# Products of the two layers of a conv mixture of experts: alternating by nine matmuls in place of by 27

## The reference, cut to what matters

```python
B, C, H, W = (32, 384, 28, 28)
E, HID, K = (4, 384, 2)
scores = jax.nn.softmax(x_flat @ gate_w + gate_b, -1)
top_v, top_i = jax.lax.top_k(scores, K)
top_w = jax.nn.softmax(top_v, -1)
...
coef = jnp.einsum('ke,kbhw->ebhw', present.astype(x.dtype), wmap)
hdn = jax.nn.relu(jnp.einsum('bchw,edc->ebdhw', x, w1) + b1[:, None, :, None, None])
y = jnp.einsum('ebdhw,eod->ebohw', hdn, w2) + b2[:, None, :, None, None]
out = jnp.einsum('ebohw,ebhw->bohw', y, coef)
...
x = x + _L0_conv_ref(_gn(x), ...)
```

## Time and profile before

| | |
|---|---|
| time, median of 3 runs | 2565.67 us (2565.27 to 2566.45) |
| time of the profiled execution | 2567.38 us |
| its span, first to last instruction | 2565.6 us |
| granted TensorE clock, mean | 0.996 |
| PE busy | 2519.3 us (98%), 13266 matmuls |
| DVE busy | 1623.8 us (63%) |
| ACT busy | 630.7 us (25%) |
| HBM | 73 GB/s over the span |

### The profile page before, as it was taken

How to read it: one execution, slowest core, us unless ns; L and a number is a source line. 1 busy time by engine, 2 the same in 40 slices (tenths; PEclk the granted TensorE clock), 3 DMA queues, 4 the chain that set the end, 5 groups by cost and what they waited for, 6 DMA issues and landing times.

```text
span 2565.6 us, 34840 instructions
## 1 busy us (share of the span) xinstructions
PE 2519.3 (98%) x13266; PEld 2302.0 (90%) x13266; DVE 1623.8 (63%) x3293; ACT 630.7 (25%) x973; POOL 74.4 (3%) x44
## 2 busy tenths in 40 slices
PE   4899999999999999999999999999999999999999
PEld 3799999999999999999999999999999999999998
DVE  7766666666666657665666666576666666665643
ACT  3322222222222222222222222222222222222211
POOL 3000000000000000000000000000000000000000
PEclk9999999999999999999999999999999999999999
DMA  4322123222133221232311322203322123231120
GB/s 161 89 78 71 52 70 89 78 82 59 52 89 93 67 79 55 69 100 68 92 55 46 100 78 82 80 25 97 89 71 78 51 72 100 61 91 51 46 75 22
DMA packets 193439, 190.15 MB, mean 74 GB/s; under 512 B 29808, under 2 KB 191856, under 8 KB 193264
## 3 DMA queue, kind: packets, MB, share of 16 engines
q1 hardware_dynamic: 193264, 187.81, 25.7%
HBM read 146.03 MB, written 41.75 MB: 73 GB/s over the span
## 4 chain that ended last, share of the span: by engine, by line
PE 96%; DVE 2%; DMA 1%; issue 1%; POOL 0%; ACT 0%; SPq 0%; DVEq 0%; POOLq 0%; ACTq 0%
PE y_ps L479 16%; PE y_ps L481 16%; PE z_ps L460 16%; PE y_ps L480 16%; PE z_ps L462 16%; PE z_ps L461 16%; PE g_ps L344 1%; DMA b_sb<-in_b 0%; DMA rows<-rows_dram 0%; DVE h_lo L519 0%; DVE x_part L323 0%; DVE x_lo L335 0%; POOL w_lo L847 0%; DVE x_raw L303 0%; DMA rows_dram<-wrow 0%
## 5 line engine op out<-in xcount | busy, mean ns | idle before, releaser
L508 DVE SCALAR_TENSOR_TENSOR hid<-z_ps,b_sb,rows 128x448 f32<-128x448 f32 x668 | 453.5, 679 | 753.9 <-PE z_ps L462 739.7
L479 PE MATMUL y_ps<-h_lo,w_hi 128*128 128x448 f32 x2016 | 741.8, 368 | 13.4 <-DVE h_lo L519 13.1
L460 PE MATMUL z_ps<-x_lo,w_hi 128*128 128x448 f32 x2016 | 743.4, 369 | 1.3 <-DVE x_lo L335 1.0
L481 PE MATMUL y_ps<-h_hi,w_hi 128*128 128x448 f32 x2016 | 741.1, 368 | 0.0
L480 PE MATMUL y_ps<-h_hi,w_lo 128*128 128x448 f32 x2016 | 740.9, 368 | 0.0
L462 PE MATMUL z_ps<-x_hi,w_hi 128*128 128x448 f32 x2016 | 736.7, 365 | 0.0
L461 PE MATMUL z_ps<-x_hi,w_lo 128*128 128x448 f32 x2016 | 736.5, 365 | 0.0
L515 ACT ACTIVATE h_hi<-hid 128x448 fp32r<-128x448 f32 x672 | 385.2, 578 | 1356.8 <-DVE hid L508 1343.2
L519 DVE SCALAR_TENSOR_TENSOR h_lo<-hid,h_hi 128x448 fp32r<-128x448 f32 x672 | 413.6, 616 | 26.5 <-ACT h_hi L515 26.1
L479 PEld LDWEIGHTS y_ps<-h_lo,w_hi 128*128 128x128 f32 x2016 | 379.3, 188 | 50.4 <-DVE h_lo L519 14.4
L460 PEld LDWEIGHTS z_ps<-x_lo,w_hi 128*128 128x128 f32 x2016 | 379.9, 188 | 38.0 <-issue 7.1
(11 more groups left out here) (97 smaller groups left out, 695.6 us busy)
## 6 DMA issues: line engine op xcount, KB each, us to landing
rows<-rows_dram SPq DMA_DIRECT2D x78, 560.0 KB, 7.4
x_raw<-in_x SPq DMA_DIRECT2D x62, 588.0 KB, 7.4
res<-in_x SPq DMA_DIRECT2D x80, 336.0 KB, 3.5
out<-res SPq DMA_DIRECT2D x78, 336.0 KB, 3.1
rows<-rows_dram SPq DMA_DIRECT2D x16, 840.0 KB, 7.2
res<-in_x SPq DMA_DIRECT2D x16, 504.0 KB, 5.8
out<-res SPq DMA_DIRECT2D x16, 504.0 KB, 6.0
rows<-rows_dram SPq DMA_DIRECT2D x16, 280.0 KB, 6.6
```

The source lines that it names most:

```text
L460: nc.tensor.matmul(z, w1_hi[:, e, j, ks], lo, start=(j == 0), stop=False)
L479: nc.tensor.matmul(y, w2_hi[:, e, k, ms], h_lo[:, slot], start=first, stop=False)
L481: ins = nc.tensor.matmul(y, w2_hi[:, e, k, ms], h_hi[:, slot], start=False, stop=last)
L508: nc.vector.scalar_tensor_tensor(hid[:, q % HIDS], z_ps[:, q % ZB, 0:T], b1_sb[:, e, k:k + 1], coef, ALU.add, ALU.mult).then_inc(scaled, 1)
```

## The change

`mm2` takes the chunks that it is to do, and PE's loop goes over chunks: nine matmuls of `mm1` for chunk c of unit u + 1, and then nine of `mm2` for chunk c of unit u. unit_done is still signalled after a unit's last matmul. Lines behind the edit move up by one (`add_product` is L534 before and L533 after).

```diff
-        def mm2(pe, G, u):
+        def mm2(pe, G, u, chunks):
             t, e = divmod(u, E)
             tail = G.last and u == UNITS - 1
...
-            for k in range(NK):
+            for k in chunks:
...
-            if tail:
-                return
-            ins.then_inc(unit_done, 1)
+                if k == NK - 1 and not tail:
+                    ins.then_inc(unit_done, 1)
...
-                    if u < UNITS - 1:
-                        if not (G.first and u == 0):
-                            mm1(pe, G, u + 1, chunks=range(2 if G.first and u == 1 else 0, NK))
-                    elif not G.last:
-                        mm1(pe, after, 0)
-                    mm2(pe, G, u)
+                    for c in range(NK):
+                        if u == UNITS - 1:
+                            if not G.last:
+                                mm1(pe, after, 0, chunks=[c])
+                        elif not (G.first and (u == 0 or u == 1 and c < 2)):
+                            mm1(pe, G, u + 1, chunks=[c])
+                        mm2(pe, G, u, [c])
```

## The result

The alternating kernel takes 2606.7 us (median of 4 runs, 2604.68 to 2607.51) against 2565.47 for the kernel before: a ratio of 1.0156, 95% interval 1.0144 to 1.0169. The forecast was 2606. The profiled execution has a span of 2605.7 us.

The account below looks back on a forecast made before the run. PE was taken as the bound, going from matmul to matmul without waits. Border waits of 15.3, 11.3 and 8.8, the first group's 3.7 and clock's 1.6 made 40.7 us on 2565.67: 2606 us, range 2590 to 2626 (8 in 10).

Parts of the forecast that it names:

- The mechanism: At tile borders PE's next product waits for DVE's add_product, late behind preparation: 2596 to 2616 us, 68 in 100.
- The waits: PE at borders into tiles 1, 2 and 5: 2.18, 1.41 and 1.25 us each, about 23 times.
- C: DVE's time from scale of a tile's third chunk to add_product: 4.84, 4.07, 3.91 us; PE waits C - 2.66.
- the term of 0.83 us: At a border, PE's product starts 0.83 us behind the start of a late add_product.
- the first group: At its border into tile 1, PE does nine matmuls instead of 27 before its wait; 18 left cost 3.7 us.
- The clock: After the first group's wait of 4 us, 3.2 us at half clock lose 1.6 us; nothing at other waits.
- the clock falls at every wait in tile 1: Rival: half clock after each wait in tile 1, 2617 us, or 2628 if down twice as long; 10 in 100.
- the 1.72 us: PE idle ahead of 76.58 in the start, after which the clock stayed at 1.00; other waits were taken as nearer this.
- The pace: Speed of matmuls following each other on PE: no change, about 10 us each way; rivals faster 10, slower 8 in 100.
- The rival on the other side: DVE finishes work ahead of add_product in time at tile borders, so no waits: 2560 to 2568 us, 4 in 100.

Follow-up runs that it names:

- the first experiment: Alternating kernel with DVE's preparation ahead of add_product (tiles 1 to 6) done in the next chunk, behind add_product: 2563.74 us, ratio 0.9987 to the kernel before.
- the fourth: Alternating kernel with one more DVE reduction of 1152 elements ahead of add_product in tiles 3, 4 and 6: 2628.98 us, ratio 1.0245 to the kernel before.
- the third: Alternating kernel put back to 27 and 27 except in each tile's first unit, which alternates by nine: 2573.76 us, ratio 1.0025 to the kernel before.
- the sixth: Alternating kernel with the two products yielding to each other after three matmuls in place of nine: 2754.74 us, ratio 1.0744 to the kernel before.
- the second experiment: Alternating kernel with PE back to 27 and 27 in each tile's first unit only: 2564.6 us, ratio 0.9991 to the kernel before.
- the seventh: Kernel before (27 and 27) with DVE's preparation put behind add_product: 2566.01 us, ratio 1.0000 to the kernel before.

## Why the prediction was right

- **The mechanism** was right: nothing but `add_product` behind DVE's preparation. The first experiment takes that work away and the loss goes; the fourth adds some and it grows; the third leaves work and distance and gives z early, and it goes; the sixth follows the same reckoning.
- **The waits** were forecast as 23 in tiles 1, 2 and 5, and 23 there are. C was right within 0.03 us in all three borders shown; in tile 1 it is 4.72 us, not 4.87, in four of the seven groups. The size was a little high, because the term of 0.83 us from the start of `add_product` to the product was read from the one case there was, in the first group. There and in the last group, which is also written out, it is 0.83 after the change too; in the six groups of the loop it is 0.74. So the three waits shown are 2.16, 1.37 and 1.16 us (the gaps less 0.20), not 2.18, 1.41 and 1.25. In the sum: 34.5 us by the waits' view, of which 30.6 lie behind the first group; this view counts from the modelled end of a matmul, 0.17 us later than its follower could start, so 22 x 0.17 = 3.7 more, 34.3 us. 35.4 were forecast.
- **The first group** lost its 18 matmuls, 3.7 us, as forecast: PE has nine behind it at 113.44 where it had 27 at 115.69.
- **The clock** was the mis-sized term. 1.6 us were put down for one stretch of 3.2 us; there were two stretches, the first twice as long. 15 matmuls in the 5.46 us from 113.44 and 10 in 3.2 us: at 0.2046 us each they would take 3.07 and 2.05, so the stretches cost an estimated 2.4 + 1.2 = 3.6 us. The second stretch is the rival "the clock falls at every wait in tile 1", come true once in seven: the waits there, of up to 2.0 us, were not as safe as the 1.72 us that they were likened to.
- **The pace** was put at no change, with 10 us each way, and changed by far less: the second experiment alternates in three quarters of the units at no cost, and the windows of the seventh point to a gain of some 2 us.
- **What the sum leaves.** 34.3 + 3.7 + 3.6 = 41.6, and the spans differ by 40.1. The two executions differ already at the start: PE's first matmul, ahead of any alternation, comes after a wait for ACT of 22.2 us before and of 18.5 us after. Counted from the first product of tile 1 (115.69 and 113.44) to the end, they take 2449.9 and 2492.3 us, which is 42.4 us more and leaves 0.8. One term that the forecast lacked is larger than that: the follower of a product that waited starts 0.31 us behind it (751.30 to 751.61), not 0.20, so 22 waits cost some 2.4 us more. The faster pace would take most of that back.
- **Luck.** That 2606 was met to within 1 us is in part luck: the waits came to 1.1 us less than forecast, the clock to 2.0 us more.
- **The rival on the other side**, that DVE is in time, is what the first experiment builds: at C = 1.13 the time is 2564 us.

## What to carry to other kernels

Before the grain of two alternating streams is made finer, work out for every single buffer both distances, from its last producer to its next, and from the release of whatever its reader's engine must do first; a finer grain takes from both, and an in-order engine with a lump of other work just ahead of the read then comes late. An engine that is busy 63% of the time can be late by 2 us at one place, and a cure is then to move the lump behind the read, which cost nothing here and gave back all 41 us. In this case the waits could be sized to within 0.2 us from the kernel before, by adding up durations from the row where the reader's chain starts.

## What was not expected of the hardware

The granted clock answers to waits of nearly the same length unevenly. In the alternating kernel seven waits of 1.8 to 2.0 us in tile 1 brought half clock once. In the kernel that alternates by three, all 17 waits of 3.6 to 4.4 us did, two of the six of 3.46 us, and five of the 23 between 1.7 and 2.2 us. So the loss from one of the shorter waits is the wait itself, and now and then an estimated 1 to 2 us more, and the length of the wait doesn't say at which.
